# An attention loop on one core: the shift's transposes one step earlier, the gather one step later

## The reference, cut to what matters

```
xn = layer_norm(x, g1, b1)
q, k, v = heads of xn @ Wq, xn @ Wk, xn @ Wv            # 4 x 16 x 256 x 16
scores = einsum('bhqd,bhkd->bhqk', q, k) / sqrt(16)
attn = softmax(scores, axis=-1)
o = einsum('bhqk,bhkd->bhqd', attn, v)
x = x + concat(o) @ Wo
```

## Time and profile before

| | us |
|---|---|
| median of 3 executions | 1475.11 |
| lowest and highest | 1474.99, 1478.46 |
| the profiled execution, time | 1474.99 |
| the profiled execution, span | 1473.2 |
| PE busy over the span | 1393.4 (95%) |
| DVE busy | 1060.1 (72%) |
| ACT busy | 926.3 (63%) |
| POOL busy | 296.2 (20%) |
| mean granted TensorE clock | 0.981 of 2.4 GHz |

### The profile page before, as it was taken

The page is one execution under the profiler, slowest core; times in us unless marked ns, Lnnn a source line. Parts: engine busy times, 40 slices in busy tenths (PEclk is TensorE's granted clock), DMA queues, the critical chain, the costliest instruction groups (busy, mean ns, idle before and its releaser), DMA issues.

```text
span 1473.2 us, 28015 instructions
## 1 busy us (share of the span) xinstructions
PE 1393.4 (95%) x11090; PEld 839.2 (57%) x11090; DVE 1060.1 (72%) x2122; ACT 926.3 (63%) x1915; POOL 296.2 (20%) x333
## 2 busy tenths in 40 slices
PE   7799999999999999999999999799999998789898
PEld 5355555555555555555555554465558997646565
DVE  5787777787777787777788884476757775757667
ACT  5367776777776777776777777225876554438621
POOL 3363212222212222212220000300021101220110
PEclk9899999999999999999999999999979999979999
DMA  6965574375574375574363520603003312065000
GB/s 188 167 143 143 112 135 84 75 132 116 115 135 84 74 131 119 112 135 83 74 119 67 86 44 1 191 29 87 1 22 100 98 32 69 18 142 118 2 0 29
DMA packets 95587, 133.12 MB, mean 90 GB/s; under 512 B 8864, under 2 KB 70944, under 8 KB 89504
## 3 DMA queue, kind: packets, MB, share of 16 engines
q1 hardware_dynamic: 95456, 131.33, 41.1%
HBM read 94.08 MB, written 37.22 MB: 89 GB/s over the span
## 4 chain that ended last, share of the span: by engine, by line
PE 73%; DVE 9%; ACT 8%; issue 5%; DMA 3%; POOL 1%; SPq 1%; DVEq 0%; POOLq 0%; ACTq 0%
PE psum L545 16%; PE psum L526 13%; PE psum L510 13%; ACT probs L765 4%; PE psum L573 3%; PE psum L612 2%; PE psum L1882 2%; PE psum L270 2%; PE psum L1908 2%; PE psum L2613 2%; PE psum L1438 2%; DVE peaks L669 2%; PE psum L279 1%; PE psum L2623 1%; PE psum L1452 1%
## 5 line engine op out<-in xcount | busy, mean ns | idle before, releaser
L669 DVE TENSOR_REDUCE peaks<-psum 128x1 f32<-128x512 f32 x1024 | 641.0, 682 | 193.2 <-PE psum L510 192.9
L765 ACT ACTIVATE probs<-psum 128x512 f32<-128x512 f32 x1024 | 525.4, 619 | 66.1 <-PE psum L526 62.3
L526 PE MATMUL psum<-queriesT,keysT 98*128 98x256 bf16 x2048 | 393.3, 274 | 7.9 <-ACT queriesT L828 3.1
L510 PE MATMUL psum<-keysT,queriesT 96*128 96x512 bf16 x1024 | 389.0, 382 | 10.2 <-DMA keysT<-key_parts 7.2
L526 PEld LDWEIGHTS psum<-queriesT,keysT 98*128 98x128 bf16 x2048 | 172.4, 99 | 202.7 <-ACT probs L765 83.9
L545 PE MATMUL psum<-probs,values 128*17 128x256 f32 x4096 | 245.9, 380 | 1.1 <-ACT probs L765 1.1
L545 PEld LDWEIGHTS psum<-probs,values 128*17 128x17 f32 x4096 | 107.2, 97 | 103.7 <-issue 26.8
L510 PEld LDWEIGHTS psum<-keysT,queriesT 96*128 96x128 bf16 x1024 | 98.4, 96 | 82.3 <-issue 52.2
L896 POOL CAST key_parts<-key_f 128x512 bf16<-128x512 f32 x57 | 34.7, 609 | 515.3 <-ACT key_f L798 507.7
L798 ACT ACTIVATE key_f<-psum,bk 128x512 f32<-128x512 f32 x59 | 40.5, 686 | 117.9 <-PE psum L573 117.8
L1712 ACT ACTIVATE weights<-psum,peaks 128x256 f32<-128x256 f32 x128 | 58.7, 487 | 21.6 <-DVE peaks L1588 20.8
(11 more groups left out here) (307 smaller groups left out, 1678.1 us busy)
## 6 DMA issues: line engine op xcount, KB each, us to landing
keysT<-key_parts SPq DMA_DIRECT2D x31, 768.0 KB, 7.8
key_parts<-key_parts SPq DMA_DIRECT2D x90, 256.0 KB
keysT<-key_parts SPq DMA_DIRECT2D x31, 512.0 KB, 10.0
ctx_nat<-in_ctx_dram SPq DMA_DIRECT2D x32, 256.0 KB, 3.6
keysT<-key_parts SPq DMA_DIRECT2D x31, 256.0 KB, 11.6
ctx_in<-in_ctx_dram SPq DMA_DIRECT2D x24, 256.0 KB, 5.8
ctx_turned<-ctxT SPq DMA_DIRECT2D x24, 256.0 KB, 4.3
ctx_T<-ctx_turned SPq DMA_DIRECT2D x12, 512.0 KB, 3.7
```

The lines of the kernel that those rows point to most:

```text
L510: e.matmul(ps, self.queriesT[0:ROWS, u % 2, g * GH + j, t * P:(t + 1) * P], self.keysT[0:ROWS, i % RING, j, c * BANK:(c + 1) * BANK], star ...
L526: made = e.matmul(ps[:, j * S:(j + 1) * S], self.keysT[0:AUG, i % RING, j, kt * P:(kt + 1) * P], self.queriesT[0:AUG, u % 2, g * GH + j, : ...
L669: e.tensor_reduce(self.peaks[:, i % 2, pair, c:c + 1], k.ps(("max", n)), AX.X, ALU.max).then_inc(*self.peaked.up(n))
L765: e.activation(self.probs[:, t % RINGP, e2 * GH * S:(e2 + 1) * GH * S], k.ps(("scores", t, e2)), ACT.Exp).then_inc(*self.exped.up((t, e2)))
```

## The change

In each iteration the shift of group g+1 moves from behind the pair of j = 1 to behind the pair of j = 0, and the gather of group g-2 moves from there to behind the pair of j = 1.

```
@@ -2491,10 +2491,10 @@
                 if g + self.AHEAD < GROUPS6:
                     yield "max", QUADS * (g + self.AHEAD) + j
                 yield "scores", QUADS * g + j
-                if j == 0 and g >= 2:
+                if j == 0 and g + 1 < GROUPS6:
+                    yield "shift", g + 1
+                if j == 1 and g >= 2:
                     yield "gather", g - 2
-                if j == 1 and g + 1 < GROUPS6:
-                    yield "shift", g + 1
                 if j == 2 and g >= 1:
                     yield "values", g - 1
```

## The result

Over 20 executions each, the changed kernel took 1481.3 us (median; 1475.0 to 1485.1) and the kernel before 1472.3 us (1467.9 to 1480.3). The ratio is 1.0053, 95% interval 1.0039 to 1.0068: slower by 7.8 us, between 5.7 and 10.0. The two medians lie 9.0 apart, which is within that. The profiled execution of the changed kernel took 1473.9 us with a span of 1472.1, a little *less* than the profiled one of before. The row of the granted clock on each page, in tenths for 40 slices, says why.

A forecast was written before the change was run, and what follows sets the result against it. TensorE was taken to bound the loop, and the earlier shift to wait for VectorE's chain, about 0.59 us in each of nine iterations. Stalls of 5.95 us on 1474.99 gave 1480.9 us, range 1478.6 to 1485.

The forecast's parts named there:

- What bounds the loop: Last attention's loop: TensorE busy all 3.89 us of an iteration, without waits; VectorE 3.30 and ScalarE 3.44 close behind.
- The length of the chain: In the loop, from the j = 3 maximum's start through VectorE's reduce and cast to the subtraction's end: 1.53 us.
- take-up of VectorE's result by TensorE: At the shift: TensorE starts 0.05 us after VectorE's subtraction ends, so the shift is ready 1.58 after the maximum's start.
- The upper bound: Most the loop's stall could cost: 0.1 more per wait for late take-up, full price in iterations 1 and 14; 7.5 us.
- The sum: Loop's stalls: 5.3 us in iterations 2 to 10, 0.4 in 1, 0.15 after 10, 0.1 in 14; together 5.95.
- ScalarE at nothing: In the loop, the shift's earlier copy on ScalarE leaves values a slack of 0.25 us: cost 0, gain at most 0.2.
- The gather at nothing: Gather one pair later in the loop: 0.39 us wherever it stands, input older than needed, so cost 0.
- The baseline: Whole program before the change: the profiled execution's 1474.99 us, to which the predicted stall was added.
- A: Behind the loop, one slow TensorE stretch less at the 2.48 us stop saves about 2 us: 1479 us, chance 0.10.
- B: In the loop, brief stops lower TensorE's clock, half speed in about one iteration of three: 1492.6 us, chance 0.05.
- C: In the loop, ScalarE becomes the bound as values wait for the shift's late copy: 1481 to 1483.6 us, chance 0.05.
- D: At the j = 0 shift, no wait and the earlier shift relieves ScalarE; not slower: 1474.8 us, chance 0.05.

The follow-up runs named there:

- the shift earlier still: Changed kernel with the shift moved one more pair earlier, ahead of the j = 0 pair: 1480.5 us, ratio 1.0081 to the kernel before.
- AHEAD = 3: Changed kernel with the maxima made three groups ahead instead of two, four more maxima ahead of the loop: 1478.4 us, ratio 1.0027 to the kernel before.

## Why the prediction was right, point by point

The time lay in the range, the direction and the mechanism held; one term of the sum was too small.

**What bounds the loop** was right: TensorE has no gap before, and VectorE's chain from the last maximum to the shift as what comes next. The length of the chain (1.53 predicted, 1.54 measured), the reduce's start 0.43 after its maximum, and the 2.90 from the shift to the next maximum (1342.81 to 1345.71) came out.

**The term that was mis-sized** is the take-up of VectorE's result by TensorE: 0.05 in the sum, 0.14 to 0.15 in iterations 3 to 11. I took it from a place where the later result was the only thing in question, although the order of the changed kernel names two semaphores at the shift. So the step came out at 4.59 instead of 4.48. The upper bound held just this 0.1, and the experiment with one semaphore less shows that it is the second semaphore.

**The sum**, iteration by iteration, from the starts of the shifts: iterations 1 and 2 cost 0.85 together (forecast 0.99; iteration 1 was the one too high, 0.26 instead of 0.4), 3 to 10 cost 5.6 (4.7), 11 cost 0.25 (0.15), 12 and 13 nothing (0), 14 about 0.06 (0.1). Together 6.7 to 6.8, instead of 5.95. The executions say 7.8 with an interval of 5.7 to 10.0, so the last microsecond is neither shown nor excluded.

**ScalarE at nothing** was right in the even part. The copy started at 1343.45, 0.64 after the shift, ended at 1344.47, and values started at 1344.72: the slack of 0.25. That values would never wait for the copy was wrong in iteration 14, where no maxima stand between: the values at 1388.13 wait 0.17 for it. The sum had 0.1 there from just this. The experiment with the gather alone shows the price where that slack is missing.

**The gather at nothing** was right for the whole change, in part by luck, and would have been wrong for the gather alone. I costed it by what it waits for, and not by what it covers: VectorE's reading of the maximum's bank, 0.29 a step. In the changed kernel the shift stands in its place and covers that.

**The baseline** was 2.7 us high: the forecast was built on an execution of 1474.99 us, while the median of 20 is 1472.3. That the predicted 1480.9 and the measured 1481.3 are so close is luck: a baseline too high stands beside a difference too small, 5.95 against 7.8.

**The rivals.** A (a slow stretch less behind the loop) did not come in the profiled execution: the same stop of 2.48, the same 0.66. But it exists: in the traces of two experiments the same stop left the clock at 1.00, and that was worth 1.5 us (I had put 2). B (the brief stops lower the clock) did not come: 1.00 through the loop. The Trainium skill ("TensorE: Matmul & The Clock Gate", section "A second HAM failure mode: psum-queue depth-cycling") reports a kernel whose clock swung under brief and frequent stops. This trace does not agree with it: the clock stayed at 1.00 with a stop of 0.6 us in every iteration. C came in the gather-alone kernel, and in this one only with the 0.17 of iteration 14. D fell: with 0.98 of work ahead of the shift against 1.53 of chain there was nothing to relieve.

## What to carry to other kernels

Where an engine that runs its instructions in order has no gaps, each job in its row also covers the time that another engine needs for its part. Before moving one, list what becomes ready behind it (here the maxima's numbers and the bank that VectorE must read), and count the work that is left ahead of each, not only the dependencies of the job that moves. Once the work between a producer and its consumer falls below the latency of the chain, a closed loop loses the difference in every turn. And read such effects in the steps of the loop: here the clock ahead of the loop moved one profiled execution against the other by as much as the whole change.

## What the hardware showed that I had not expected

- A second semaphore at an instruction, fulfilled long before, put 0.09 us on TensorE's take-up of the one that came last: 0.14 to 0.15 with two, 0.05 to 0.06 with one (step 4.59 against 4.50).
- The same stop of 2.48 us, behind the same work, was followed by values of 1.91 us at a lowered clock in before and in the changed kernel, and of 1.06 at the full clock in two others (the shift earlier still, and AHEAD = 3). In four more the clock fell while the values ran or behind them (1.22 to 1.74). So the stop's length alone does not decide it; what does is not shown. Stops of 0.5 to 1.1 us in every iteration never lowered it in the loop.
- The same instructions ahead of the loop took 36.1 or 39.2 us in two executions, with the same idle time of TensorE (6.6), so by the clock (0.87 and 0.79).
- Eight narrow transposes and the values behind them overlap when they follow one another directly: in the kernel with the shift at j = 2 the first values are recorded 0.22 after the shift's start, and both together took 1.40 where they took 1.63 before.
